# Turning all four q tiles on VectorE through DRAM, two beats later, in an attention and FFN kernel

## The chip, the cores and the metric

The kernel runs on one core of a Trainium2 chip. The metric is device time in microseconds (us) of one execution, lower is better. A core has TensorE (matrix products, PE in the profile, its weight loads PEld), VectorE (DVE), ScalarE (ACT), GpSimd (POOL) and SyncE (SP, here an issuer of DMAs). Each engine works through its own list of instructions in order; between engines the kernel sets semaphores by hand.

## The reference, cut to what matters

For each of 16 batches x is 128 x 1024 and the context 128 x 1024 (channels by positions), with 8 heads of 64.

```python
xn = layernorm(x)                                    # over the 1024 positions
q  = softmax(Wq @ xn, over the 64 channels of a head) * 64 ** -0.5
k  = softmax(Wk @ ctx, over the positions)
out = Wo @ (context of k and Wv @ ctx, applied to q) + bo
x  = x + out / norm(out over the 128 channels) * g * sqrt(128)
x  = x + ffn(layernorm(x))                           # gated lookup in 256 slots
```

## The kernel before, in words

About the first four fifths of the time are a pipeline of batches. `PERIODS` = 19 periods b run over every engine's list, each of four beats i = 0 to 3. In period b the keys of batch b are made, the queries of p = b-1, and older batches o = b-2 and e = b-3 are finished; the order on each engine is written out by hand in the loops at L672 (TensorE), L908 (ScalarE), L1133 (GpSimd) and L1417 (VectorE).

A beat on VectorE: `k_turn` (L1217, a block transpose of the exponentials of keys), `k_maximum` (L1210, straight from the PSUM buffer `k_slot`), `q_reciprocal` (L1242 `qsum`, L1246 `qrec`) for the queries one tile back, in two of four beats `q_block_turn` (L1255), and `q_shift` (L1229 `qm`, L1235). Between `q_shift` and `q_reciprocal` of a tile ScalarE does `q_exponential` (L798); after `q_reciprocal` GpSimd does `q_scale` (L1056). In beat 0 VectorE also makes the mean and variance of x (`x_statistics`, L1196, L1200), from which GpSimd's `rstd_pow` (L1039 to L1046) makes scale and bias for `x_layernorm`.

A q tile must be turned (queries down, channels across) before the output product. Tiles 0 and 1 (`BY_BLOCKS`) are turned in blocks of 32 by VectorE into `qt`, written to DRAM by one DMA on SP (`q_out`, L413) and read back by four DMAs that ScalarE issues (`q_in`, L814). Tiles 2 and 3 (`BY_PE`) are turned by TensorE (`q_turn`, L501) into the PSUM buffer `turn` and copied by ScalarE (`q_copy`, L803).

Then `o_pair` (L548) makes the output of two position tiles in `ob`; ScalarE copies it (`o_copy`, L824) and sums squares (`o_square`, L834, four small instructions, into the one buffer `l2`); GpSimd's `norm_scale` makes 1/norm from `l2` (L1067 `l2c`, L1069 `rn`) and scales (L1071 `o_sb`); TensorE turns it back (`o_turn`, L559); ScalarE takes it from PSUM (`o_scale`, L843); GpSimd adds it to x (`residual`, L1077); ScalarE and GpSimd make the second layernorm's numbers (`square_sum` L851, `rstd2_pow` L1089 to L1098). SP also moves the turned keys, sixteen DMAs for a half (`move_k`, L405, `ekT<-kt`). TensorE's other work in a beat is `k_tile` and `q_pair` (L475 to L477), `g_part` (L517) and `m_product` (L526). In the last two periods the steps of the FFN (`hidden_step`) begin.

One wait matters below: the first lines of `o_square`, and where the count `rn_pow` that it waits for is made, in `norm_scale`:

```python
act.wait_ge(o_copied, 2 * b + half + 1)
wait(act, rn_pow, b)
...
nc.gpsimd.tensor_tensor(rn[:, :], l2c[:, :], half_neg[:, 0:J], ALU.pow).then_inc(rn_pow, 1)
```

Of the kernel before, what the change touches and what calls it, by code (L numbers as in the profile page):

```python
# [49 lines left out]


def turned_by_pe(b, i):

    return len(BY_PE) * b + sum(t <= i for t in BY_PE)


def attention_ffn_kernel(nc, x, ctx_rows, ctx_cols, WqT_raw, WkT_raw, Wv_rows, WoT_rows, bo_row, g_col, Wuq_cols,
# [3 lines left out]
    with ctx:  # L61
# [46 lines left out]
        rstd = sb("rstd", [P, 1])
        nb = sb("nb", [P, 1])
        mr = sb("mr", [P, 1])  # L110
        mr2 = sb("mr2", [P, 1])
# [19 lines left out]
        q_turned = nc.dram_tensor("q_turned", (2, P, QUAD, T * P), F32, kind="Internal").ap()  # L131
# [340 lines left out]
        def _(pe):  # L472
# [24 lines left out]
            def q_turn(b, i):  # L497
                pe.wait_ge(q_mul, 4 * b + i + 1)
                for t in range(T):
                    for n in range(2):  # L500
                        last = nc.tensor.transpose(turn[:, (2 * t + n) * P:(2 * t + n + 1) * P],  # L501
# [1055 lines left out]
```

## Time and profile before

| | us |
|---|---|
| median of 3 runs | 637.53 (637.11 to 642.76) |
| the profiled execution | 638.21, span 636.4, mean granted TensorE clock 0.99 |
| busy in the span: PE, DVE | 598.8, 540.2 |
| busy in the span: ACT, POOL | 419.1, 409.8 |
| chain that ended last, shares | PE 36%, DVE 25%, POOL 16%, issue 14% |

The table's busy times are sums over the whole span. The rows further down show single instructions: start and duration in us from the start of the span, the engine (with q for its queue, where a DMA is issued), the line of the kernel and the operation, what it writes <- what it reads, and in brackets how long the engine stood idle before it and whom it waited for. Starts follow each other in less than a duration where an engine overlaps the end of one instruction with the next.

### The profile page before, as it was taken

How to read it: one execution, taken by the hardware profiler on the slowest of the kernel's cores; microseconds unless marked ns; L12 is line 12 of the kernel's file. 1: busy time of each engine (PE TensorE's matmuls, PEld its weight loads, DVE VectorE, ACT ScalarE, POOL GpSimd, SP SyncE). 2: the span in 40 equal slices, each digit the busy share in tenths (PEclk: the TensorE clock that was granted, in tenths of full speed). 3: DMA queues.
4: the chain of work that ended last, by engine and by line, in shares of the span. 5: the costliest groups of instructions: out<-in, count | busy, mean ns of one | idle time of the engine just before them, and what ended most of it. 6: DMA issues, size and time to landing. Idle time of an engine off the chain costs nothing.

```text
span 636.4 us, 11451 instructions
## 1 busy us (share of the span) xinstructions
PE 598.8 (94%) x3718; PEld 517.3 (81%) x3718; DVE 540.2 (85%) x721; ACT 419.1 (66%) x864; POOL 409.8 (64%) x421
## 2 busy tenths in 40 slices
PE   4989999999999999999999999999997799999896
PEld 3768888888888888888888888888886799998574
DVE  5999998989989898989898989899985635756897
ACT  5556657667667676767676676676683556774783
POOL 4964476777676778777777777776673536421394
PEclk9999999999999999999999999999998899999899
DMA  8849695867778684959595858675582500000056
GB/s 300 230 137 242 183 221 167 208 185 193 192 184 213 161 226 140 252 157 238 152 239 163 217 167 208 184 195 162 143 251 43 169 15 2 2 2 0 35 231 264
DMA packets 63530, 106.11 MB, mean 167 GB/s; under 512 B 11392, under 2 KB 43680, under 8 KB 61168
## 3 DMA queue, kind: packets, MB, share of 16 engines
q1 hardware_dynamic: 53216, 84.84, 46.1%
q10 hardware_dynamic: 9360, 18.09, 12.5%
q0 software_dynamic: 896, 2.45, 1.3%
q8 instruction: 30, 0.49, 0.3%
q14 instruction: 28, 0.23, 0.2%
HBM read 46.62 MB, written 25.17 MB: 113 GB/s over the span
## 4 chain that ended last, share of the span: by engine, by line
PE 36%; DVE 25%; POOL 16%; issue 14%; DMA 3%; SPq 3%; ACT 2%; DVEq 0%; POOLq 0%; ACTq 0%
DVE qsum L1242 7%; PE ob L548 7%; DVE kt L1217 5%; DVE qm L1229 5%; POOL ctx_lo L1033 4%; PE gm L604 4%; PE turn L604 4%; PE gm L517 4%; POOL qs_sb L1056 4%; POOL o_sb L1071 3%; POOL rn L1069 3%; SPq L405 3%; DVE qt L1255 3%; DMA ekT<-kt 2%; PE turn L559 2%
## 5 line engine op out<-in xcount | busy, mean ns | idle before, releaser
L1056 POOL TENSOR_TENSOR qs_sb<-qs_sb,qrec 128x1024 f32<-128x1024 f32 x64 | 121.9, 1905 | 126.0 <-DVE qrec L1246 125.9
L548 PE MATMUL ob<-mt_sb,q_hd 128*128 128x128 f32 x1024 | 127.4, 278 | 4.5 <-POOL mt_sb L1062 2.8
L548 PEld LDWEIGHTS ob<-mt_sb,q_hd 128*128 128x128 f32 x1024 | 122.6, 193 | 9.3 <-issue 6.4
L517 PE MATMUL gm<-ekT,ctxT 128*128 128x256 f32 x512 | 120.6, 384 | 4.7 <-DMA ekT<-kt 4.7
L517 PEld LDWEIGHTS gm<-ekT,ctxT 128*128 128x128 f32 x512 | 97.5, 192 | 22.3 <-DMA ekT<-kt 7.6
L788 ACT ACTIVATE ek<-k_slot,nkm 128x1024 f32<-128x1024 f32 x62 | 69.1, 1114 | 61.5 <-DVE nkm L1210 61.4
L798 ACT ACTIVATE qs_sb<-qs_sb 128x1024 f32<-128x1024 f32 x64 | 67.9, 1061 | 51.3 <-DVE qs_sb L1235 50.9
L1210 DVE TENSOR_REDUCE nkm<-k_slot 128x1 f32<-128x1024 f32 x62 | 74.1, 1194 | 25.1 <-PE k_slot L477 24.9
L1242 DVE TENSOR_REDUCE qsum<-qs_sb 128x16 f32<-128x1024 f32 x64 | 77.1, 1205 | 4.8 <-ACT qs_sb L798 3.7
L1235 DVE TENSOR_TENSOR qs_sb<-q_slot,qm 128x1024 f32<-128x1024 f32 x64 | 78.3, 1224 | 2.2
L1217 DVE STREAM_TRANSPOSE kt<-ek 128x1024 f32<-128x1024 f32 x64 | 79.0, 1234 | 0.8 <-DMA ekT<-kt 0.8
L1229 DVE TENSOR_REDUCE qm<-q_slot 128x16 f32<-128x1024 f32 x64 | 76.0, 1187 | 1.3 <-PE q_slot L477 1.1
L475 PE MATMUL k_slot<-ctx_hi,WkT_hi 128*128 128x512 f32 x124 | 54.5, 439 | 8.9 <-DVE ctx_lo L1408 7.2
L475 PE MATMUL q_slot<-WqT_hi,xn_hi 128*128 128x512 f32 x128 | 53.0, 414 | 0.8 <-DVE qs_sb L1235 0.8
L477 PE MATMUL q_slot<-WqT_lo,xn_hi 128*128 128x512 f32 x128 | 50.2, 392 | 0.0
L476 PE MATMUL q_slot<-WqT_hi,xn_lo 128*128 128x512 f32 x128 | 50.0, 390 | 0.0
L477 PE MATMUL k_slot<-ctx_lo,WkT_hi 128*128 128x512 f32 x124 | 49.3, 397 | 0.0
L476 PE MATMUL k_slot<-ctx_hi,WkT_lo 128*128 128x512 f32 x124 | 49.0, 396 | 0.0
L1050 POOL TENSOR_TENSOR xn_lo<-xn,xn_hi 128x1024 fp32r<-128x1024 f32 x16 | 38.3, 2392 | 4.3 <-ACT xn_hi L782 4.3
L1255 DVE STREAM_TRANSPOSE qt<-qs_sb 128x1024 f32<-128x1024 f32 x32 | 38.0, 1186 | 0.0
L834 ACT ACTIVATE junk<-o_sb 128x128 f32<-128x128 f32 x128 | 37.6, 299 | 0.0
L803 ACT COPY q_hd<-turn 128x1024 f32<-128x1024 f32 x32 | 31.9, 998 | 8.1 <-PE turn L501 8.1
(208 smaller groups left out, 1290.8 us busy)
## 6 DMA issues: line engine op xcount, KB each, us to landing
ekT<-kt SPq DMA_DIRECT2D x496, 64.0 KB, 3.1
q_turned<-qt SPq DMA_DIRECT2D x16, 1024.0 KB, 4.8
q_hd<-q_turned ACTq DMA_DIRECT2D x64, 256.0 KB, 6.0
ctx_in<-ctx_rows SPq DMA_DIRECT2D x16, 512.0 KB, 6.2
x_all<-x SPq DMA_DIRECT2D x16, 512.0 KB, 4.8
ctxT<-ctx_cols SPq DMA_DIRECT2D x16, 512.0 KB, 6.2
out<-q_hd SPq DMA_DIRECT2D x15, 512.0 KB, 2.6
Wuq_in<-Wuq_cols ACTq DMA_DIRECT2D x1, 1280.0 KB, 6.4
```

The lines of the kernel that those rows point to most:

```text
L475: nc.tensor.matmul(dst, lhs[0], rhs[0], start=True, stop=False)
L476: nc.tensor.matmul(dst, lhs[1], rhs[0], start=False, stop=False)
L477: return nc.tensor.matmul(dst, lhs[0], rhs[1], start=False, stop=True)
L517: last = nc.tensor.matmul(gm[:, cols], ctxT[:, b % 2, j, :], ekT[:, 2 * half:2 * half + 2, :, j * BLK:(j + 1) * BLK], start=(j == 0), stop ...
L548: last = nc.tensor.matmul(ob[:, (j % 4) * C:(j % 4 + 1) * C], q, mt_sb[:, b % 2, t, :], start=(t == 0), stop=(t == T - 1))
L788: nc.scalar.activation(ek[:, i % 2, :], k_psum(b, i)[:, :], ACT.Exp, bias=nkm[:, i:i + 1], accum_out=ksum[:, b % 2, i:i + 1]).then_inc(k_e ...
L1056: nc.gpsimd.tensor_tensor(e, e, qrec[:, i % 2, :].unsqueeze(2).broadcast_to([P, PAIR, DH]), ALU.mult).then_inc(q_mul, 1)
L1210: V.tensor_reduce(nkm[:, i:i + 1], k_psum(b, i)[:, :], AX, ALU.max, negate=True).then_inc(k_max, 1)
L1217: V.transpose(kt[:, i, :], ek[:, i % 2, :]).then_inc(k_T, 1)
L1229: V.tensor_reduce(qm[:, :], q, AX, ALU.max).then_inc(q_max, 1)
L1235: V.tensor_tensor(qs_sb[:, i % 2, :].rearrange("p (m d) -> p m d", d=DH), q, qm[:, :].unsqueeze(2).broadcast_to([P, PAIR, DH]), ALU.subtra ...
L1242: V.tensor_reduce(qsum[:, :], qs_sb[:, i % 2, :].rearrange("p (m d) -> p m d", d=DH), AX, ALU.add).then_inc(q_sum, 1)
```

## The change

All four q tiles are turned in blocks by VectorE and go through DRAM in two pairs (h = 0: tiles 0 and 1, h = 1: tiles 2 and 3), each with its own write and its own four reads; `qt` is shared by the pairs. `q_turn` and `q_copy` go. The output pairs run two beats later (pairs 0 and 1 in beats 2 and 3, pairs 2 and 3 in beats 0 and 1 of the next period), and what follows them moves too: `o_copy`, `o_square`, `norm_scale` (now in GpSimd's beat 0, for f = b-4), `o_turn`, `o_scale`, `residual`, `square_sum`, `rstd2_pow`. The sum and the sum of squares of x come from ScalarE (`x_sum`, `x_square`) for batches 2 to 15, with a negated mean by GpSimd (`x_negate`), in place of VectorE's `x_statistics`; x is loaded one period earlier. Small single columns share one tile. The diff, cut to its core (12 spaces of indentation left out):

```diff
-def q_out(b):
-    sp.wait_ge(q_blocks, 2 * b + 2)
-    wait(sp, q_back, 16 * QUAD * (b - 1))
-    sp.dma_start(q_turned[b % 2].rearrange("p q x -> p (q x)"),
-                 qt[:, :, :].rearrange("p i x -> p (i x)")).then_inc(q_written, 16)
+def q_out(b, h):
+    sp.wait_ge(q_blocks, 4 * b + 2 * h + 2)
+    wait(sp, q_back[h], 16 * QUAD * (b - 1))
+    sp.dma_start(q_turned[b % 2, h].rearrange("p q x -> p (q x)"),
+                 qt[:, :, :].rearrange("p i x -> p (i x)")).then_inc(q_written[h], 16)
 def ffn_tables():
...
         load_ctxT(b)
     if has(b):
         move_k(b, 0)
     if has(b - 1):
-        q_out(b - 1)
+        q_out(b - 1, 0)
     if 2 <= b + 2 < B:
         load_ctx(b + 2)
     if has(b):
         move_k(b, 1)
     if b == B:
         ffn_tables()
+    if has(b - 1):
+        q_out(b - 1, 1)
...
-def o_pair(b, n_out):
-    i = OUT_ORDER[n_out]
-    if i in BY_BLOCKS:
-        pe.wait_ge(q_back, 16 * QUAD * (b + 1))
-    else:
-        pe.wait_ge(q_copied, turned_by_pe(b, i))
-    if n_out == 0:
+def o_pair(b, i):
+    if i % 2 == 0:
+        pe.wait_ge(q_back[i // 2], 16 * QUAD * (b + 1))
+        wait(pe, o_copied, 2 * b + i // 2)
+    if i == 0:
         pe.wait_ge(mt_biased, b + 1)
         if b == 0:
             pe.wait_ge(score_ready, 2)
-    if n_out % 2 == 0:
-        wait(pe, o_copied, 2 * b + n_out // 2)
...
         if b == 1 and i == 1:
             value_products(1)
             router_product()
-        qb, qi = (p, i - 2) if i >= 2 else (o, i + 2)
-        if has(qb) and qi in BY_PE:
-            if qb == 0 and qi == BY_PE[0]:
-                pe.wait_ge(u_done, 1)
-                pe.wait_ge(ident_in, 16)
-            take_turn(q_turn, qb, qi)
-            q_turn(qb, qi)
         if has(p):
             if p == 0 and i == 0:
...
                 m_product(p)
-        if has(e) and i == 2:
-            take_turn(o_turn, e)
-            o_turn(e)
-        if has(o):
-            o_pair(o, i)
+        at, n = (o, i - 2) if i >= 2 else (e, i + 2)
+        if has(at):
+            o_pair(at, n)
+        if has(f) and i == 1 or b == B + 2 and i == 3:
+            take_turn(f if i == 1 else B - 1)
+            o_turn(f if i == 1 else B - 1)
         if b == 0 and i == 3:
             head_products()
...
+def x_sum(b):
+    act.wait_ge(x_in[b % 4], 16 * (b // 4 + 1))
+    wait(act, x_negated, b - 2)
+    wait(act, l2_sum, 2 * (b - 4) + 1)
+    wait(act, x_squared, b - 2)
+    wait(act, ssq_done, b - 5)
+    nc.scalar.activation(junk[:, :, :].rearrange("p j c -> p (j c)"), X[:, b, :], ACT.Copy,
+                         accum_out=xsum).then_inc(x_summed, 1)
+def x_square(b):
+    act.wait_ge(x_negated, b - 1)
+    wait(act, x_ve, b)
+    wait(act, l2_sum, 2 * (b - 4) + 2)
+    act.wait_ge(x_summed, b - 1)
+    nc.scalar.activation(junk[:, :, :].rearrange("p j c -> p (j c)"), X[:, b, :], ACT.Square, bias=nm1,
+                         accum_out=xsq).then_inc(x_squared, 1)
...
-def q_copy(b, i):
-    act.wait_ge(q_T, turned_by_pe(b, i))
-    wait(act, o_prod, 4 * (b - 1) + OUT_ORDER.index(i) + 1)
-    nc.scalar.copy(q_hd[:, i, :], turn[:, :]).then_inc(q_copied, 1)
...
-def q_in(b):
-    if b == 0:
+def q_in(b, h):
+    if b == 0 and h == 0:
         act.wait_ge(k_weights, 2)
         act.wait_ge(q_weights, 2)
         act.wait_ge(u_prod, 1)
-    act.wait_ge(q_written, 16 * (b + 1))
-    wait(act, o_prod, 4 * b)
+    act.wait_ge(q_written[h], 16 * (b + 1))
+    wait(act, o_prod, 4 * (b - 1) + 2 * h + 2)
     for q in range(QUAD):
-        nc.scalar.dma_start(q_hd[q * BLK:(q + 1) * BLK, 0:2, :].rearrange("r i (a x) -> r (i a) x", a=2),
-                     q_turned[b % 2, :, q, :].rearrange("(a r) x -> r a x", a=QUAD)).then_inc(q_back, 16)
+        nc.scalar.dma_start(q_hd[q * BLK:(q + 1) * BLK, 2 * h:2 * h + 2, :].rearrange("r i (a x) -> r (i a) x", a=2),
+                            q_turned[b % 2, h, :, q, :].rearrange("(a r) x -> r a x",
...
     act.wait_ge(o_copied, 2 * b + half + 1)
     wait(act, rn_pow, b)
     wait(act, l2_sum, 2 * b + half)
-    first = 2 * OUT_ORDER[2 * half]
-    for j in range(first, first + 4):
-        last = nc.scalar.activation(junk[:, j % 4, :], o_sb[:, b % 2, j, :], ACT.Square,
+    if half == 0:
+        wait(act, x_squared, min(b + 2, B - 2))
+    else:
+        wait(act, x_summed, min(b + 3, B - 2))
+        wait(act, ssq_done, min(b - 1, RESIDUAL_BY_VECTOR))
+    for j in range(4 * half, 4 * half + 4):
+        last = nc.scalar.activation(junk[:, j, :], o_sb[:, b % 2, j, :], ACT.Square,
                                     accum_out=l2[:, j:j + 1])
...
     act.wait_ge(x1_done, b + 1)
     act.wait_ge(nm2_done, b + 1)
     wait(act, ve2_done, b)
-    nc.scalar.activation(o_sb[:, b % 2, :, :].rearrange("p j c -> p (j c)"), X[:, b, :], ACT.Square,
+    act.wait_ge(l2_sum, 2 * (b + 2) + 1)
+    nc.scalar.activation(junk[:, :, :].rearrange("p j c -> p (j c)"), X[:, b, :], ACT.Square,
                          bias=nm2[:, b % 2:b % 2 + 1], accum_out=ssq[:, :]).then_inc(ssq_done, 1)
...
 for b in range(PERIODS):
-    p, o, e = b - 1, b - 2, b - 3
+    p, o, e, f = b - 1, b - 2, b - 3, b - 4
     for i in range(4):
-        if i == 0 and o == B - 1:
-            q_copy(o, 2)
         if i == 0 and has(o):
             mt_scale(o)
         if i == 0 and has(e):
+            o_copy(e, 0)
+        if i == 2 and has(e):
             o_copy(e, 1)
-        if i == 2 and has(o):
-            o_copy(o, 0)
+        if i == 2 and 0 <= f < RESIDUAL_BY_VECTOR:
+            o_scale(f)
         if i == 1 and has(o):
-            q_in(o)
-        qb, qi = (p, i - 1) if i else (o, 3)
-        if has(qb):
-            q_exponential(qb, qi)
-        qb, qi = (p, i - 2) if i >= 2 else (o, i + 2)
-        if has(qb) and qi in BY_PE and (qb, qi) != (B - 1, 2):
-            q_copy(qb, qi)
+            q_in(o, 0)
+        if i == 3 and has(o):
+            q_in(o, 1)
         if b == B + 1 and i == 0:
             act.wait_ge(q_prod, 4 * B)
             act.wait_ge(m_prod, B)
             hT_high(0, 0)
             h_scale(1, 1)
+        qb, qi = (p, i - 1) if i else (o, 3)
+        if has(qb):
+            q_exponential(qb, qi)
         if 0 < b < B:
             k_exponential(b, i)
         if i == 1 and 0 < b and has(b + 1):
             ctx_high(b + 1)
         if i == 0 and has(e):
+            o_square(e, 0)
+        if i == 3 and has(e) and e < B - 1 or i == 2 and e == B - 1:
             o_square(e, 1)
-        if i == 3 and has(o):
-            o_square(o, 0)
-        if i == 3 and 0 <= e < RESIDUAL_BY_VECTOR:
-            o_scale(e)
         if i == 1 and 0 < b < B:
             x_layernorm(b)
-        if i == 1 and 0 <= e - 1 < RESIDUAL_BY_VECTOR:
-            square_sum(e - 1)
+        if i == 1 and 0 <= f - 1 < RESIDUAL_BY_VECTOR:
+            square_sum(f - 1)
         if i == 2:
             if has(p):
                 g_copy(p)
             if 0 < b < B:
                 x_high(b)
+            if 1 < b + 1 < B:
+                x_sum(b + 1)
+        if i == 3 and 1 < b + 1 < B:
+            x_square(b + 1)
         if b == 1 and i == 0:
             act.wait_ge(u_prod, 1)
             nc.scalar.mul(U[:, :, :].rearrange("p h c -> p (h c)"), turn[:, :],
...
+def x_negate(b):
+    pool.wait_ge(x_summed, b - 1)
+    nc.gpsimd.tensor_scalar(mv1[:, b, 0:1], xsum, 1.0 / N, None, ALU.mult).then_inc(x_mean, 1)
+    wait(pool, x_squared, b - 2)
+    pool.wait_ge(x_mean, b - 1)
+    nc.gpsimd.tensor_scalar(nm1, mv1[:, b, 0:1], -1.0, None, ALU.mult).then_inc(x_negated, 1)
 def rstd_pow(b):
-    pool.wait_ge(x_mv, b + 1)
     wait(pool, x_norm, b)
-    nc.gpsimd.tensor_scalar(ve[:, :], mv1[:, b, 1:2], LN_EPS, None, ALU.add).then_inc(x_ve, 1)
+    if b < 2:
+        pool.wait_ge(x_mv, b + 1)
+        nc.gpsimd.tensor_scalar(ve[:, :], mv1[:, b, 1:2], LN_EPS, None, ALU.add).then_inc(x_ve, 1)
+    else:
+        pool.wait_ge(x_squared, b - 1)
+        nc.gpsimd.tensor_scalar(ve[:, :], xsq, 1.0 / N, LN_EPS, ALU.mult, ALU.add).then_inc(x_ve, 1)
     pool.wait_ge(x_ve, b + 1)
     nc.gpsimd.tensor_tensor(rstd[:, :], ve[:, :], half_neg[:, 0:1], ALU.pow).then_inc(x_rstd, 1)
...
 for b in range(PERIODS):
-    p, o, e = b - 1, b - 2, b - 3
+    p, o, e, f = b - 1, b - 2, b - 3, b - 4
     for i in range(4):
         if i == 0 and has(o):
             mt_bias(o)
-        if i == 0 and 0 <= e - 1 < RESIDUAL_BY_VECTOR:
-            residual(e - 1)
+        if i == 3 and 0 <= f < RESIDUAL_BY_VECTOR:
+            residual(f)
+        if i == 3 and 1 < b + 1 < B:
+            x_negate(b + 1)
         if i == 3 and 0 < b < B:
...
             q_scale(qb, qi)
         if i == 0 and 0 < b < B:
             rstd_pow(b)
-        if i == 0 and has(e - 1) and e - 1 >= RESIDUAL_BY_VECTOR:
-            rstd2_pow(e - 1)
-        if i == 3 and 0 <= e - 1 < RESIDUAL_BY_VECTOR:
-            rstd2_pow(e - 1)
+        if i == 0 and has(f):
+            norm_scale(f)
+        if i == 0 and has(f - 1) and f - 1 >= RESIDUAL_BY_VECTOR:
+            rstd2_pow(f - 1)
+        if i == 2 and 0 <= f - 1 < RESIDUAL_BY_VECTOR:
+            rstd2_pow(f - 1)
         if i == 1 and b > 0 and has(b + 1):
             ctx_low(b + 1)
-        if i == 1 and has(e):
-            norm_scale(e)
+        if b == B + 2 and i == 3:
+            norm_scale(B - 1)
         if b == B and i == 3:
             for half in range(2):
                 pool.wait_ge(k_moved[half], moved(B))
             nc.gpsimd.memset(q_rows[:, :, BOT:P], 1.0).then_inc(query_ones, 1)
         if early_step(b, i) > 0:
             hidden_sum(early_step(b, i))
-rstd2_pow(B - 1)
+for b in range(B - 2, B):
+    rstd2_pow(b)
...
 def q_block_turn(b, i):
-    n = BY_BLOCKS.index(i)
     dve.wait_ge(q_mul, 4 * b + i + 1)
-    wait(dve, q_written, 16 * b)
+    wait(dve, q_written[1 - i // 2], 16 * (b + i // 2))
     turned = qt[:, :, :].rearrange("p i x -> p (i x)").rearrange("p (q t i n x) -> p i n t q x", q=QUAD, t=T,
                                                                  i=2, n=2)
-    V.transpose(turned[:, n, :, :, :, :],
+    V.transpose(turned[:, i % 2, :, :, :, :],
                 qs_sb[:, i % 2, :].rearrange("p (n t q x) -> p n t q x", n=2, t=T,
                                              q=QUAD)).then_inc(q_blocks, 1)
...
             q_reciprocal(qb, qi)
-        if i == 0 and 0 < b < B:
+        if i == 0 and b == 1:
             x_statistics(b)
         if i == 1:
             if has(p):
                 k_scale(p)
         qb, qi = (p, i - 2) if i >= 2 else (o, i + 2)
-        if has(qb) and qi in BY_BLOCKS:
+        if has(qb):
             q_block_turn(qb, qi)
         if has(p):
             q_shift(p, i)
-        if i == 2 and has(e) and e >= RESIDUAL_BY_VECTOR:
-            residual(e)
-        if i == 3 and has(e) and e >= RESIDUAL_BY_VECTOR:
-            statistics(e)
+        if i == 2 and has(f) and f >= RESIDUAL_BY_VECTOR:
+            residual(f)
+        if i == 3 and has(f) and f >= RESIDUAL_BY_VECTOR:
+            statistics(f)
         if b == 0 and i == 3:
             dve.wait_ge(side_in, 16 * 2)
             V.tensor_scalar_mul(bo_bc[:, :], bo_bc[:, :], 0.5).then_inc(bo_halved, 1)
```

## Rows read from the trace of the kernel before

**Rows 1.** Chain that ended last, 240 to 345: start, us, engine, tile, line

```profile
303.88 1.91 POOL o_sb L1071
```

**Rows 2.** Timeline, VectorE, 299 to 331 (columns as told above)

```profile
299.66 1.23 DVE L1217 STREAM_TRANSPOSE kt<-ek 128x1024 f32<-128x1024 f32 x1
...
310.19 1.23 DVE L1210 TENSOR_REDUCE nkm<-k_slot 128x1 f32<-128x1024 f32 x1 [1.95 <-PE k_slot L477]
311.34 1.21 DVE L1242 TENSOR_REDUCE qsum<-qs_sb 128x16 f32<-128x1024 f32 x1
312.58 0.25 DVE L1246 RECIPROCAL qrec<-qsum 128x16 f32<-128x16 f32 x1
312.75 1.19 DVE L1255 STREAM_TRANSPOSE qt<-qs_sb 128x1024 f32<-128x1024 f32 x1
...
318.49 1.20 DVE L1242 TENSOR_REDUCE qsum<-qs_sb 128x16 f32<-128x1024 f32 x1
...
329.70 1.23 DVE L1217 STREAM_TRANSPOSE kt<-ek 128x1024 f32<-128x1024 f32 x1
```

**Rows 3.** Timeline, GpSimd, 299 to 331

```profile
301.78 0.26 POOL L1067 TENSOR_SCALAR l2c<-l 128x8 f32<-128x8 f32 x1
302.13 1.68 POOL L1069 TENSOR_TENSOR rn<-l2c,half_neg 128x8 f32<-128x8 f32 x1
...
312.91 1.90 POOL L1056 TENSOR_TENSOR qs_sb<-qs_sb,qrec 128x1024 f32<-128x1024 f32 x1 [2.93 <-DVE qrec L1246]
...
320.13 1.91 POOL L1056 TENSOR_TENSOR qs_sb<-qs_sb,qrec 128x1024 f32<-128x1024 f32 x1
322.12 0.23 POOL L1039 TENSOR_SCALAR ve<-mv 128x1 f32<-128x1 f32 x1
...
323.35 0.23 POOL L1046 TENSOR_SCALAR nb<-mr 128x1 f32<-128x1 f32 x1
```

**Rows 4.** Timeline, ScalarE, 299 to 331 (ACTq: a DMA issue)

```profile
301.02 1.06 ACT L798 ACTIVATE qs_sb<-qs_sb 128x1024 f32<-128x1024 f32 x1
...
318.97 0.83 ACTq L814 DMA_DIRECT2D q_hd<-q_turned  x2
...
320.33 0.46 ACTq L814 DMA_DIRECT2D q_hd<-q_turned  x1
```

**Rows 5.** Timeline, ScalarE, 436 to 441

```profile
438.74 1.11 ACT L788 ACTIVATE ek<-k_slot,nkm 128x1024 f32<-128x1024 f32 x1 [0.30 <-DVE nkm L1210]
439.11 0.98 ACTq L814 DMA_DIRECT2D q_hd<-q_turned  x2
```

**Rows 6.** Line 413 between 434 and 435: the write, issue to landing

```profile
L413 SPq DMA_DIRECT2D q_turned<-qt x1: 332/332/332, 434.1 to 434.1; - x1
...
DMA to landing us min/median/max: 3.8/3.8/3.8
```

**Rows 7.** Timelines, TensorE, 299 to 331 and 455 to 530

```profile
301.54 3.61 PE L517 MATMUL gm<-ekT,ctxT 128*128 128x256 f32 x16
...
308.53 0.47 PE L475 MATMUL k_slot<-ctx_hi,WkT_hi 128*128 128x512 f32 x1
...
310.00 0.40 PE L475 MATMUL q_slot<-WqT_hi,xn_hi 128*128 128x512 f32 x1
...
482.48 5.41 PE L517 MATMUL gm<-ekT,ctxT 128*128 128x256 f32 x16 [3.77 <-DMA ekT<-kt]
...
499.51 2.94 PE L548 MATMUL ob<-mt_sb,q_hd 128*128 128x128 f32 x16 [2.83 <-POOL mt_sb L1062]
...
509.64 2.05 PE L548 MATMUL ob<-mt_sb,q_hd 128*128 128x128 f32 x16 [1.10 <-ACT q_hd L803]
```

**Rows 8.** Three stretches: us, busy (instructions) by engine, PEclk, DMA share, GB/s

```profile
483.00:486.00 3.00, 3.00 (x9) 2.43 (x8) 0.93 (x1) 0.00 (x0) 0.00 (x0) 0.56 0.00 0
500.00:503.00 3.00, 3.00 (x17) 2.80 (x17) 1.86 (x2) 3.00 (x10) 0.61 (x1) 0.57 0.39 157
510.00:515.00 5.00, 5.00 (x42) 5.00 (x41) 1.23 (x1) 2.37 (x3) 3.93 (x3) 1.00 0.06 13
```

More of the change, by code:

```diff
@@ L26 @@
 MOVED = 16 * QUAD * QUAD
-BY_BLOCKS = (0, 1)
-BY_PE = tuple(i for i in range(4) if i not in BY_BLOCKS)
-OUT_ORDER = BY_PE + BY_BLOCKS
 RESIDUAL_BY_VECTOR = B - 3
@@ L103, in attention_ffn_kernel @@
         nm2 = sb("nm2", [P, 2])
-        ssq = sb("ssq", [P, 1])
-        ve = sb("ve", [P, 1])
-        ve2 = sb("ve2", [P, 1])
         l2c = sb("l2c", [P, J])
[L108 to L111, printed above, removed]
+        singles = sb("singles", [P, 10])
+        ssq, ve, ve2, rstd, nb, mr, mr2, xsum, nm1, xsq = (singles[:, n:n + 1] for n in range(10))
         att = ExitStack()
@@ L128, in attention_ffn_kernel @@
         att.close()
[L131 removed]
+        q_turned = nc.dram_tensor("q_turned", (2, 2, P, QUAD, T * P), F32, kind="Internal").ap()
         stage = q_hd[:, :, :].rearrange("p t n -> p (t n)")
@@ L242, in attention_ffn_kernel @@
         log_rel_in = sem("log_rel_in")
-        x_in = [sem(f"x_in{k}") for k in range(2)]
+        x_in = [sem(f"x_in{k}") for k in range(4)]
         ctx_loaded = sem("ctx_loaded")
@@ L296, in attention_ffn_kernel @@
         q_mul = sem("q_mul")
-        q_T = sem("q_T")
-        q_copied = sem("q_copied")
         q_blocks = sem("q_blocks")
-        q_written = sem("q_written")
-        q_back = sem("q_back")
+        q_written = [sem(f"q_written{h}") for h in range(2)]
+        q_back = [sem(f"q_back{h}") for h in range(2)]
         o_back = sem("o_back")
@@ L495, in q_pair @@
                 last.then_inc(q_prod, 1)
[L497 to L501, printed above, removed]
-                                                   qs_sb[:, i % 2, n * HALF + t * P:n * HALF + (t + 1) * P],
-                                                   ident[:, :])
-                last.then_inc(q_T, 1)
             def g_part(b, half, js):
@@ L819, in o_copy @@
                 wait(act, x1_done, b - 1)
-                if half == 0:
-                    wait(act, ssq_done, min(b - 1, RESIDUAL_BY_VECTOR))
                 wait(act, l2_sum, 2 * b)
-                first = 2 * OUT_ORDER[2 * half]
-                nc.scalar.copy(o_sb[:, b % 2, first:first + 4, :],
+                nc.scalar.copy(o_sb[:, b % 2, 4 * half:4 * half + 4, :],
                                ob[:, :].rearrange("p (j c) -> p j c", c=C)).then_inc(o_copied, 1)
@@ L1230, in q_shift @@
                 dve.wait_ge(q_max, n + 1)
-                if n >= 2 and (n - 2) % 4 in BY_PE:
-                    dve.wait_ge(q_T, turned_by_pe((n - 2) // 4, (n - 2) % 4))
-                if n >= 2 and (n - 2) % 4 in BY_BLOCKS:
-                    dve.wait_ge(q_blocks, len(BY_BLOCKS) * ((n - 2) // 4) + BY_BLOCKS.index((n - 2) % 4) + 1)
+                wait(dve, q_blocks, n - 1)
                 V.tensor_tensor(qs_sb[:, i % 2, :].rearrange("p (m d) -> p m d", d=DH), q,
```

54 lines of the change are left out of this document (25 added, 29 removed).

## The prediction

> **What bounds the kernel now.** I read four views in this order: the chain that ended last, to see which engines hand work to each other; VectorE's own timeline, to see whether it ever stands still; the timelines of ScalarE and GpSimd, for what each link of a chain costs; and the stretches in which TensorE's granted clock falls. The profiled execution took 638.21 us, its span 636.4; the median of the runs is 637.53, so a sum against the profiled execution is lowered by 0.7 at the end.
>
> Batches overlap, and the loop over periods b repeats: from one `k_turn` of beat 2 to the same one a period later are 30.04 us (299.66 to 329.70) [rows 2]. VectorE is the fullest engine in it. It stands still at one place, 1.95 us ahead of `k_maximum` in beat 3, for TensorE's `k_tile` [rows 2]. The chain shows why TensorE is late there: in beat 2 it waits for GpSimd's `norm_scale` (o_sb, to 305.78) before `o_turn` [rows 1], and `o_pair` and `k_tile` are queued behind that. So a period is VectorE's own work, 28.1 us, plus that stall of 1.95.
>
> **The change, part by part.** I write b for the period, p, o, e, f for b-1 to b-4.
>
> *VectorE.* Two more block turns a period (tiles 2 and 3), 1.19 us each [rows 2]; away goes `x_statistics`. A beat with a block turn and no wait runs from one `qsum` to the next in 7.15 us (311.34 to 318.49) [rows 2]; afterwards all four beats are of that kind, 4 x 7.15 = 28.6. TensorE loses both `q_turn`s, and its beat 2 no longer holds `o_turn`, so the stall of 1.95 before `k_maximum` should go but for a few tenths. Were this all, a period would fall by 1.4 us.
>
> *What is hidden.* ScalarE gives up two `q_copy` and takes `x_sum` and `x_square`: in beats 2 and 3, behind exponentials with slack of some tenths of a us, at nothing. GpSimd's `x_negate` and its other steps that move to other beats: GpSimd waits for VectorE in most beats, nothing, with one exception below. The second pair's write on SP is queued behind the sixteen `move_k` DMAs of the half before it and can leave about when the turn of tile 3 ends; the next turn into the same buffer comes over 5 us later, and the whole buffer (both tiles at once, as now) was written in 3.8 where I looked [rows 6]. Nothing, and up to 0.5 a period if traffic slows it.
>
> *The exception: one wait in ScalarE's queue.* `o_square` waits for `rn_pow >= b` of its batch, that is for `norm_scale` of the batch before, because both use the one buffer `l2`. Now both `o_square`s find that long done. In the changed kernel `o_square(e, 0)` is issued in beat 0 of period b, and the batch before e is f, whose `norm_scale(f)` moves to GpSimd's beat 0 of the same period, behind `q_scale(o, 3)` and `rstd_pow(b)`. `q_scale(o, 3)` in turn needs VectorE's `qrec` of that same beat. Behind the blocked `o_square` stand, in ScalarE's order, the four DMA issues of `q_in(o, 0)` and then `q_exponential(p, 0)`, and for the last VectorE waits in beat 1 with `qsum`. So there is a closed loop through three engines, from `qsum` of beat 0 to `qsum` of beat 1:
> - `qsum` start to `qrec` start 1.24 (311.34 to 312.58) [rows 2], on to `q_scale` 0.33 (312.91) [rows 3]: 1.57;
> - `q_scale` to GpSimd's next instruction 1.99 (320.13 to 322.12) [rows 3];
> - `rstd_pow`, four small instructions, 322.12 to 323.35 + 0.23 [rows 3]: 1.46, and 0.1 to the next;
> - `l2c` and `rn`, 301.78 to 302.13 + 1.68 [rows 3]: 2.03, and 0.1 to reach ScalarE;
> - ScalarE hands out the squares and then issues the four `q_in` DMAs. Now the same sequence lies behind a `k_exponential`: the first DMA is issued 0.37 after that one starts (438.74 to 439.11) [rows 5], and the four issues last from 318.97 to 320.33 + 0.46 [rows 4]: 0.37 + 1.82 = 2.19, and 0.1 to the next;
> - `q_exponential` 1.06 [rows 4] and 0.05 to `qsum`.
>
> The sum is 1.57 + 1.99 + 1.56 + 2.13 + 2.29 + 1.11 = 10.65, where VectorE's own work between the two places is 7.15. VectorE is stalled for 3.5 us in beat 1. A period then takes 10.65 + 3 x 7.15 = 32.1 us against 30.04: 2.1 more. The other beats cannot win it back, since they hold nothing but VectorE's work.
>
> The length of the ScalarE link is the one that is open. If the DMA issues delayed nothing, four squares at about 0.3 each (1.2 us) would stand in place of 2.19, and the period were 31.1. Against that: in a later period the write that `q_in` waits for left at 434.1 and landed 3.8 later, at 437.9 [rows 6], yet the first `q_in` DMA was issued only at 439.11, behind the `k_exponential` ahead of it that had to wait for its data until 438.74 [rows 5]. ScalarE's queue does not run past an instruction that waits, so I take 2.19. The Trainium skill, "Perfetto Trace Analysis", section "DVE / Act Engine Instruction", says that the sequencer pushes an engine instruction into a wait queue and is free for the next one while the semaphores are awaited. By that rule the DMAs would be issued during the wait, and the period would be the shorter one; the rows just named speak against it here.
>
> *TensorE's clock.* The stall opens a gap for TensorE. `k_exponential(b, 1)` (1.11 [rows 5]) follows the late `q_exponential`, then `k_tile(b, 2)` (1.47, 308.53 to 310.00 [rows 7]) ends about 2.6 us after `qsum`; the next product needs `q_shift` of beat 1, some 5.0 after `qsum`. So TensorE idles about 2.4 us in one piece. Around gaps of 3.77 and 2.83 us [rows 7] the granted clock stood at 0.56 and 0.57 in the stretch that followed, so it was mostly at the lower of its two levels, 1.2 GHz; after one of 1.10 (at 509) [rows 7] it kept 1.00, the level of 2.4 GHz [rows 8]. A gap of 2.4 lies between these, nearer to 2.83. The price of one fall: sixteen matmuls of `g_part` took 5.41 where they take 3.61 [rows 7], 1.8 more, and these stand in beat 2, where TensorE has no slack. Bounds: no period or all twelve; I take three, 5.4 us, because the rows show falls beside longer gaps only.
>
> *How many periods.* The wait bites where e >= 1 and the products of keys still run: b = 4 to 15, twelve periods, 12 x 2.1 = 25.2. In period 3 there is no batch f and the period falls by 1.4. Period 16 waits for DMAs of `ekT` anyway (TensorE 3.77 idle [rows 7]), which covers most of the loop. In the last two periods `o_turn` of the last batch comes a beat later, and the block in ScalarE's queue holds up the first transposed hidden rows; on the other side the turns of the last tiles no longer need TensorE and ScalarE. I put these at 0, bounds -4 and +7, one loop less its cover on either side.
>
> Sum: 638.2 + 25.2 - 1.4 + 5.4 = 667.4; less 0.7 for the median: **667 us**.
>
> **The rivals.**
> 1. *The queue runs ahead* (the DMA issues are no part of the loop). Period 31.1: 12 x 1.06 - 1.4 = 11.3, three clock falls 5.4: 638.2 + 16.7 - 0.7 = 654. For it: the squares themselves need only 1.2 us. Against it: the issue at 439.11.
> 2. *The clock falls in every period.* 12 x 1.8 in place of 3 x 1.8: 667 + 16 = 683. For it: a gap of 2.4 with another short gap ahead of it is close to 2.83. Against it: each fall in the rows stands beside a longer gap.
> 3. *The loop does not close, the kernel is faster.* The place is `o_square(e, 0)`: were `norm_scale(f)` done before `qrec` of beat 0 is needed, ScalarE would pass it, VectorE would be the bound at 28.6, and thirteen periods would win 1.4 each: 638.2 - 18.7 - 0.7 = 619, or some 622 with a few tenths of stall left in each. It decides at a ScalarE link so short that the loop takes 7.15 in all, 3.5 less than the sum. Against it: the four GpSimd links alone, 1.57 + 1.99 + 1.56 + 2.13 = 7.25, already exceed it.
> 4. *No change:* the loop takes 8.6 us, so that stall and gain cancel. No row makes it so short.
>
> **How the numbers follow.** The forecast (3.5 us stall, a few clock falls) has 0.63, its own range 658 to 677; rival 1 has 0.13, rival 2 has 0.12, rival 3 has 0.08, no change 0.04. The range reaches from rival 1 with a good tail (654 - 4 = 650) to rival 2 with a bad one (683 + 5 = 688). Within 1% of the time before, 631 to 644, is about what a measurement here cannot tell from no change: slower 0.88, same 0.04, faster 0.08.
>
> **What would show it.** Right: in the profile after, ScalarE's `o_square` after beat 0 waits some 6 us for GpSimd's `rn`; VectorE's `qsum` waits about 3.5 us for `q_exponential` once a period; `k_turn` repeats every 32 us in periods 4 to 15 and faster in period 3; the 1.95 us wait of `k_maximum` is gone or a few tenths. Wrong: a period of 28.6 to 29 with `rn` done ahead of `o_square` (rival 3); `q_in` DMAs issued while ScalarE waits (rival 1); granted clock well below 1.00 across the middle (rival 2); or a wait of the block turn for the pair's write, which I put at nothing.

## The result, and the profile after

| | before | after |
|---|---|---|
| median of the runs, us | 637.96 (637.11 to 642.76, 4 runs) | 697.49 (694.77 to 698.38, 4 runs) |
| ratio to before, 95% interval | | 1.091 (1.088 to 1.095) |
| span of the profiled execution, us | 636.4 | 695.3 |
| start of period 4 to start of period 16, us | 359.6 | 407.7 |
| from there to the end, us | 171.0 | 181.3 |

The change costs 59.5 us; 667 was forecast, with a range to 688. Here and below a period runs from the `k_turn` of one beat 0 to the next. Of the 58.9 us between the spans, periods 4 to 15 hold 48.1, everything from period 16 on 10.4, and the first three periods with the start 0.4.

The page of the kernel after, its span and its engines (busy us, share of the span, instructions):

```profile
span 695.3 us, 11139 instructions
...
PE 597.0 (86%) x3462; PEld 501.4 (72%) x3462; DVE 561.2 (81%) x711; ACT 420.5 (60%) x888; POOL 417.3 (60%) x449
```

VectorE is busy for 81% of the span, where it was busy for 85% before. Its waits, 140 to 480 us (line, waited for: us in total, times, longest), say what it stands for:

```profile
DVE qsum L1234 <- ACT qs_sb L778: 34.0, 11, 4.3
DVE nkm L1205 <- PE k_slot L468: 17.1, 10, 1.8
DVE qt L1246 <- DMA q_turned<-qt: 1.2, 3, 0.7
```

The first was forecast, 3.1 us a time. The second is the wait of [rows 2], which the change was to remove: it is back with 1.7 us, for another reason. One period of VectorE's timeline (start, us, engine, line, operation; in brackets the idle time before it and what ended it), against [rows 2]:

```profile
309.20 1.23 DVE L1212 STREAM_TRANSPOSE kt<-ek 128x1024 f32<-128x1024 f32 x1
...
311.46 1.20 DVE L1234 TENSOR_REDUCE qsum<-qs_sb 128x16 f32<-128x1024 f32 x1
312.70 0.25 DVE L1238 RECIPROCAL qrec<-qsum 128x16 f32<-128x16 f32 x1
...
321.92 1.22 DVE L1234 TENSOR_REDUCE qsum<-qs_sb 128x16 f32<-128x1024 f32 x1 [2.92 <-ACT qs_sb L778]
...
337.01 1.23 DVE L1205 TENSOR_REDUCE nkm<-k_slot 128x1 f32<-128x1024 f32 x1 [1.75 <-PE k_slot L468]
...
343.04 1.24 DVE L1212 STREAM_TRANSPOSE kt<-ek 128x1024 f32<-128x1024 f32 x1
```

The period is 33.84 us instead of 30.04. GpSimd in beat 0 of it, against [rows 3]:

```profile
313.03 1.90 POOL L1046 TENSOR_TENSOR qs_sb<-qs_sb,qrec 128x1024 f32<-128x1024 f32 x1 [3.25 <-DVE qrec L1238]
315.02 0.19 POOL L1029 TENSOR_SCALAR singles<-singles 128x1 f32<-128x1 f32 x1
...
316.54 0.26 POOL L1057 TENSOR_SCALAR l2c<-l 128x8 f32<-128x8 f32 x1
316.87 1.67 POOL L1059 TENSOR_TENSOR rn<-l2c,half_neg 128x8 f32<-128x8 f32 x1
```

And ScalarE, which starts `o_square` 0.08 us after that `rn` ends, against [rows 4]:

```profile
318.62 0.31 ACT L811 ACTIVATE junk<-o_sb 128x128 f32<-128x128 f32 x1 [5.84 <-issue]
...
318.90 0.32 ACTq L789 DMA_DIRECT2D q_hd<-q_turned  x1
...
319.74 1.05 ACTq L789 DMA_DIRECT2D q_hd<-q_turned  x2
320.83 1.06 ACT L778 ACTIVATE qs_sb<-qs_sb 128x1024 f32<-128x1024 f32 x1 [0.92 <-issue]
```

That is the loop as it was written down. TensorE in beats 2 and 3 of the same period, and two stretches of it (us, busy, PEclk, DMA share, GB/s), against [rows 7, 8]:

```profile
324.34 0.39 PE L468 MATMUL k_slot<-ctx_lo,WkT_hi 128*128 128x512 f32 x1
327.11 0.50 PE L466 MATMUL q_slot<-WqT_hi,xn_hi 128*128 128x512 f32 x1 [2.38 <-DVE qs_sb L1227]
...
329.55 4.25 PE L499 MATMUL gm<-ekT,ctxT 128*128 128x256 f32 x16
```

```profile
322.00:324.00 2.00, 1.77 (x13) 1.00 1.06 241
...
327.00:330.00 3.00, 2.89 (x8) 0.57 0.99 337
```

TensorE stands for 2.38 us, and in the stretch behind that the granted clock is 0.57, mostly the 1.2 GHz level. The products of q and the first part of `g_part` go slowly, `k_tile` of beat 3 is late, and `k_maximum` waits 1.75 for it. This happens in each of the periods 5 to 15, eleven times, and not in period 4, which takes 32.2 us. Yet period 4 has the same gap, 2.38 us, and behind it the clock stays at 1.00:

```profile
124.20 0.47 PE L466 MATMUL q_slot<-WqT_hi,xn_hi 128*128 128x512 f32 x1 [2.38 <-DVE qs_sb L1227]
```

```profile
124.00:128.00 4.00, 3.80 (x17) 1.00 0.98 369
```

So the length of the gap alone does not decide; why period 4 was spared stays open.

### The profile page after: what moved, and what is told of

It reads as the page before. It is cut to its first block, busy times and chain, and to the rows that moved or that the text cites. A ratio compares the mean times of both kernels' runs of the same rounds, so it can differ in the third digit from the quotient of the medians.

```text
span 695.3 us, 11139 instructions
## 1 busy us (share of the span) xinstructions
PE 597.0 (86%) x3462; PEld 501.4 (72%) x3462; DVE 561.2 (81%) x711; ACT 420.5 (60%) x888; POOL 417.3 (60%) x449
## 3 DMA queue, kind: packets, MB, share of 16 engines
q10 hardware_dynamic: 18576, 34.87, 21.9%
## 4 chain that ended last, share of the span: by engine, by line
PE 34%; issue 27%; DVE 15%; ACT 11%; DMA 4%; ACTq 3%; SPq 3%; POOL 2%; DVEq 0%; POOLq 0%
PE gm L499 9%; PE ob L524 4%; ACT junk L811 4%; PE turn L577 4%; DVE qm L1224 3%; DVE qsum L1234 3%; ACTq L789 3%; SPq L394 3%; DVE qs_sb L1227 2%; ACT qs_sb L778 2%; DVE nkm L1205 2%; PE q_slot L466 2%; PE gm L577 2%; ACT mt_sb L837 2%; PE q_slot L468 2%
## 5 line engine op out<-in xcount | busy, mean ns | idle before, releaser
L499 PE MATMUL gm<-ekT,ctxT 128*128 128x256 f32 x512 | 127.7, 400 | 1.6 <-DMA ekT<-kt 1.4
L499 PEld LDWEIGHTS gm<-ekT,ctxT 128*128 128x128 f32 x512 | 105.0, 206 | 21.6 <-DMA ekT<-kt 3.3
L466 PE MATMUL q_slot<-WqT_hi,xn_hi 128*128 128x512 f32 x128 | 58.4, 456 | 58.8 <-DVE qs_sb L1227 58.8
L466 PEld LDWEIGHTS q_slot<-WqT_hi,xn_hi 128*128 128x128 f32 x128 | 26.0, 203 | 80.4 <-issue 76.5
L1246 DVE STREAM_TRANSPOSE qt<-qs_sb 128x1024 f32<-128x1024 f32 x64 | 76.9, 1202 | 5.8 <-DMA q_turned<-qt 5.8
L466 PE MATMUL k_slot<-ctx_hi,WkT_hi 128*128 128x512 f32 x124 | 54.5, 440 | 16.5 <-ACT ek L768 9.2
L468 PE MATMUL q_slot<-WqT_lo,xn_hi 128*128 128x512 f32 x128 | 55.7, 435 | 0.0
L467 PE MATMUL q_slot<-WqT_hi,xn_lo 128*128 128x512 f32 x128 | 55.4, 433 | 0.0
L774 ACT COPY g_sb<-gm 128x512 f32<-128x512 f32 x16 | 9.4, 586 | 51.8 <-PE gm L499 51.8
```

What stands on the lines that cost most here:

```text
L466: nc.tensor.matmul(dst, lhs[0], rhs[0], start=True, stop=False)
L467: nc.tensor.matmul(dst, lhs[1], rhs[0], start=False, stop=False)
L468: return nc.tensor.matmul(dst, lhs[0], rhs[1], start=False, stop=True)
L499: last = nc.tensor.matmul(gm[:, cols], ctxT[:, b % 2, j, :], ekT[:, 2 * half:2 * half + 2, :, j * BLK:(j + 1) * BLK], start=(j == 0), stop ...
```

## Experiments

All times are medians, with the ratio to the kernel before on the same chip. Because the first period differs between the executions (27.6 to 33.8 us, see the experiments on x's statistics), I also give the length of the twelve periods 4 to 15 in the profiled execution; before 359.6, after 407.7.

**The clock alone.** Is the second wait the clock's?

```diff
-                        k_tile(b, i)
+                        k_tile(b, i, 2 if i == 2 and b >= 4 else 1)   # computed that many times over
```

> The changed kernel, in which TensorE computes the third k tile of each batch from 4 on twice over, into the same place: 1.36 us of work put into the gap of 2.35 us ahead of the third q tile, from which VectorE reads only later. The loop stays. Theory A (the gap brings the clock down, and the lower clock costs 1.8 us a period behind it): the gap is 1.0 us, no clock falls in periods 5 to 15, k_max no longer waits in beat 3, the period is 34.05 - 1.8 = 32.2 and the time 697.5 - 11 x 1.8 = 678. Rival D (the clock falls of themselves every 34 us, whatever TensorE did before, or their cost is hidden by VectorE's work): 693 to 700.

Measured 685.71 us, ratio 1.072 (1.069 to 1.075); the twelve periods 391.6. TensorE in that gap, VectorE's waits, and the stretch 140 to 450 (us; busy us and instructions of PE, PEld, DVE, ACT, POOL; PEclk, DMA share, GB/s):

```profile
292.23 0.47 PE L466 MATMUL q_slot<-WqT_hi,xn_hi 128*128 128x512 f32 x1 [1.03 <-DVE qs_sb L1227]
...
293.69 3.62 PE L499 MATMUL gm<-ekT,ctxT 128*128 128x256 f32 x16
```

```profile
DVE qsum L1234 <- ACT qs_sb L778: 25.8, 9, 3.6
DVE qt L1246 <- DMA q_turned<-qt: 6.0, 9, 1.5
DVE nkm L1205 <- PE k_slot L468: 0.3, 2, 0.2
```

```profile
140.00:450.00 310.00, 281.90 (x1661) 234.85 (x1658) 272.45 (x275) 199.60 (x443) 213.75 (x236) 1.00 0.91 242
```

More work on TensorE makes the kernel faster. With the gap at 1.03 the clock is 1.00 throughout, `g_part` takes 3.62 instead of 4.25, `k_maximum` waits for next to nothing, and the wait of `qsum` is about as it was (2.9 us a time, 3.1 before). The twelve periods lose 16.1 us, of which the median shows 11.8 (this execution's first period was 5.0 longer). Rival D falls. What is left, 391.6 against 359.6, is the loop with little else. In eight of its twelve periods ScalarE's part of the loop, from the first square to `q_exponential`, is longer than the 2.21 above, 2.38 to 3.51, mostly because the four issues last longer; one of them:

```profile
315.98 0.31 ACT L811 ACTIVATE junk<-o_sb 128x128 f32<-128x128 f32 x1 [5.85 <-issue]
...
317.09 2.28 ACTq L789 DMA_DIRECT2D q_hd<-q_turned  x2
319.42 1.06 ACT L778 ACTIVATE qs_sb<-qs_sb 128x1024 f32<-128x1024 f32 x1 [2.15 <-issue]
```

The waits of the block turn for the write (6.0 us) cost nothing here: they stand in beat 0, inside the loop, and `qsum` waits the less behind them.

**The loop, opened.** Theory A against the write as the true end of ScalarE's wait.

```diff
-        l2 = sb("l2", [P, J])
+        l2 = sb("l2", [P, 2, J])
-                wait(act, rn_pow, b)
+                wait(act, rn_pow, b - 1)
-                        accum_out=l2[:, j:j + 1]
+                        accum_out=l2[:, b % 2, j:j + 1]
```

(`norm_scale` reads `l2[:, b % 2, :]`.)

> The changed kernel with two buffers for the sums of squares (l2 by the parity of the batch), so that o_square(e, 0) waits for rn of the batch before and no more for that of the batch just ahead of it. Nothing else is changed. Theory A (a closed loop VectorE, GpSimd, ScalarE costs 3.4 us a period from period 4 on, and the 2.35 us gap that it leaves on TensorE ahead of the third q tile costs another 1.8 by a lower clock): the semaphore wait of 6.9 us on ScalarE goes, the qsum of beat 1 no longer waits, no clock falls in periods 5 to 15, the period is 28.6 to 29.3 us against 34.0; 697.5 - 11 x 5.0 - 3.2 = 639 us, between 632 and 645. Rival B (the write of the pair to DRAM would end ScalarE's wait at the same place anyway, because q_in stands ahead of q_exp): the wait moves to the first q_in, the period stays above 33, 685 to 697 us.

Measured 656.38 us, ratio 1.028 (1.025 to 1.030); the twelve periods 366.4. VectorE's waits in 140 to 450, and that stretch:

```profile
DVE qt L1246 <- DMA q_turned<-qt: 15.3, 12, 2.6
DVE nkm L1205 <- PE k_slot L468: 0.6, 2, 0.5
```

```profile
140.00:450.00 310.00, 285.55 (x1698) 239.65 (x1697) 290.66 (x294) 215.75 (x468) 226.68 (x252) 0.99 1.02 258
```

The wait of `qsum` is gone, 34.0 us (140 to 480) to none, and with it all falls of the clock from 140 to 455 but one: 41 us of the 59.5 go with the loop. Rival B falls: the period is 30.5 on average, not above 33. But the time is 656 and not 639. Neither theory had said what takes the place: the block turn now waits for the write of the other pair, 15.3 us in twelve times, and the DMA engines' share is 1.02, that is, full. Nothing covers these waits any more: period 15, which has none, takes 28.9 us, and period 4, with one of 2.64, takes 31.7. The kernel before had 0.73 there and the kernel after 0.84.

**Two links, shortened.** `o_square` waits for the last reader of `l2` instead of `rn`; and, in another kernel, `q_in(o, 0)` stands behind `q_exponential(p, 0)`.

```diff
-                wait(act, rn_pow, b)
+                wait(act, l2_clamped, b)
```

> The changed kernel, with one wait of o_square set on l2_clamped of the batch before (the last reader of l2) instead of rn_pow, one GpSimd instruction later. Theory A: the loop is shorter by one rn (1.68 us) and still closed: 10.5 to 8.8 us against 7.15 of VectorE's own work, so the wait of qsum falls from 3.4 to 1.7 us, and TensorE's gap from 2.35 to 0.65. If the clock then stays up, the period is 34.05 - 1.7 - 1.8 = 30.5 and the time 697.5 - 11 x 3.5 - 1.7 = 657; if it falls all the same, 32.35 and 697.5 - 12 x 1.7 = 677. Rival B (the write to DRAM ends the wait): no change, 690 to 697.

```diff
-                    if i == 1 and has(o):
-                        q_in(o, 0)
...
                     if has(qb):
                         q_exponential(qb, qi)
+                    if i == 1 and has(o):
+                        q_in(o, 0)
```

> The changed kernel with the four issues of q_in(o, 0) in beat 1 put behind q_exp(p, 0) on ScalarE instead of ahead of it. Theory A: the four issues (1.9 us) leave the loop, which is 8.6 us against 7.15; the wait of qsum falls from 3.4 to about 1.5, and with the clock up the period is 30.3 (time 655), with the clock still falling 32.15 (time 675). Rival C (the queue takes the four issues ahead while ScalarE still waits or computes, so they are no part of the loop): no change, 693 to 700.

The first: 666.80 us (1.043, 1.039 to 1.048), the twelve periods 377.5, most of them 30.9. The loop in one of these:

```profile
303.16 1.20 DVE L1234 TENSOR_REDUCE qsum<-qs_sb 128x16 f32<-128x1024 f32 x1
...
312.33 1.22 DVE L1234 TENSOR_REDUCE qsum<-qs_sb 128x16 f32<-128x1024 f32 x1 [1.33 <-ACT qs_sb L778]
```

That is 9.17 instead of 10.46, 1.3 of the 1.7 of `rn`; the rest is lost because the four issues last longer (ScalarE's part is 2.68 instead of 2.21). In 140 to 450 the clock falls twice. The median is 10 above my 657: the two periods with a fall take 33.5 and 34.1, and most others stay at 30.9 where 30.5 was written.

The second: 679.64 us (1.063, 1.058 to 1.068), the twelve periods 381.7, most of them 31.2 to 31.9. The loop in one of the best:

```profile
309.44 1.20 DVE L1234 TENSOR_REDUCE qsum<-qs_sb 128x16 f32<-128x1024 f32 x1
...
318.86 1.22 DVE L1234 TENSOR_REDUCE qsum<-qs_sb 128x16 f32<-128x1024 f32 x1 [1.41 <-ACT qs_sb L778]
```

Rival C falls, but only half of the 1.9 us came: the loop is 9.42, and against the 32.2 of the kernel without falls the best periods gain 1.0. The rows of ScalarE above say why. The issues run beside the four squares, and `q_exponential` waits only the last 0.92 us for them (`[0.92 <-issue]`); the squares remain when the issues are gone. And 17.6 us of waits for the write appear; most of them stand in beat 0, where the loop covers them, but the longest, 4.3 us, stands in the longest period, 33.6.

**The transfers.** With the loop open, from batch 2 on a quarter of the second pair's bytes.

```diff
+                rows = slice(0, BLK if h and b >= 2 else P)
-                sp.dma_start(q_turned[b % 2, h] ..., qt[:, :, :] ...)
+                sp.dma_start(q_turned[b % 2, h, rows] ..., qt[rows, :, :] ...)
+                    (each of the four reads: 32 x 512 elements instead of four times that)
```

> The kernel with two buffers of sums (656 us), in which from batch 2 on the second pair of q tiles is moved only by a quarter: 32 of 128 rows are written to DRAM, and each of the four reads brings a quarter of its bytes. That leaves three quarters of that pair's values out; all other work is the same. Theory E (with the loop open, the DMA engines are full: 95% busy, 1.3 us a period of the block turn waiting for the write of the other pair, and that holds the period at 30.5 where VectorE's own work is 28.7): the wait for the write goes, the period is 28.6 to 29.2, 656 - 12 x 1.5 = 638, between 632 and 644. Rival F (not the bytes but the order of the issues on the queue of SyncE sets when a pair is written, or another engine is at its limit): 650 to 657.

Measured 637.45 us, ratio 0.997 (0.993 to 1.000); the twelve periods 349.9, eleven of them 28.9. All of VectorE's waits in 140 to 450, and that stretch:

```profile
DVE nkm L1210 <- PE k_slot L469: 0.2, 1, 0.2
```

```profile
140.00:450.00 310.00, 297.25 (x1802) 253.29 (x1799) 305.67 (x313) 227.28 (x499) 237.30 (x262) 1.00 0.82 216
```

VectorE is busy 305.7 of 310 us: this is close to the period that the prediction wrote down for the change without its loop, 28.6. So three quarters of the second pair's bytes cost 16.5 us in twelve periods (366.4 - 349.9) once nothing slower hides them. Rival F falls.

**x's statistics.** Put back on VectorE with the loop closed, and with it open; and moved alone, in the kernel before.

```diff
-                    if i == 0 and b == 1:
+                    if i == 0 and 0 < b < B:
                         x_statistics(b)
```

(with `x_sum`, `x_square`, `x_negate` and their waits taken out)

> The changed kernel with x's statistics back on VectorE, in beat 0, as before the change; the loop stays closed. Theory A (VectorE's work between qsum of beat 0 and qsum of beat 1 lies under the loop of 10.5 us, which has 3.4 us of room): the 1.4 us that VectorE gets back cost nothing, 693 to 702 us, and the wait of qsum in beat 1 is shorter by about as much. Rival G (VectorE is the bound, and the statistics' move did save): 697.5 + 12 x 1.4 = 714.

> The kernel with two buffers of sums (656 us), with x's statistics back on VectorE. Theory E (the transfers hold the period at 30.5, so that VectorE's 1.4 us are covered up to some 0.5): 656 to 664. Rival G (VectorE is the bound there, and the statistics' move saves what it takes off it): 656 + 12 x 1.4 = 673 or more.

Closed: 693.62 us (1.089, 1.081 to 1.096), 4 below the changed kernel, within what the runs of either spread; the twelve periods are 398.9 against 407.7. VectorE's own work fills some of the stall (21.9 us of waits of `qsum` in nine times, 2.4 each); TensorE's gap is then about 2.0 in most periods, and in 140 to 455 the clock falls five times instead of nine. Open: 660.38 us (1.037, 1.029 to 1.044), 4 above; the twelve periods are 365.5 against 366.4, and the block turn's waits for the write shrink from 15.3 us to 0.4: VectorE now works where it waited. In both, what the change takes off VectorE buys nothing in these periods. Rival G falls twice.

> The kernel before the change, with x's statistics alone moved to ScalarE and GpSimd as the change does it, and nothing else of the change. Theory G (VectorE is the bound of the kernel before, and nothing closes a loop here, for the sums of squares are read in the same period, beats away from the next): the period falls from 30.04 by the 1.4 to 1.5 us of the statistics to 28.6, in 14 periods, 637.5 - 14 x 1.4 = 618, between 615 and 625. Rival H (another limit stands close behind VectorE, the transfers or TensorE, as in the kernel with two buffers of sums): 630 to 638.

Alone: 630.50 us, ratio 0.987 (0.982 to 0.993), the twelve periods 347.6. The median lies in H's 630 to 638, and H names one limit rightly: in 140 to 450 VectorE waits 23.3 us for TensorE's `k_tile`, in 21 times, and the period is 28.9 and not G's 28.6. And 5.3 us are lost at the start: the first period is 33.1, where the kernel before has 27.8. So:

```diff
-                if 2 <= b + 2 < B:
-                    load_x(b + 2)
+                if 2 <= b + 1 < B:
+                    load_x(b + 1)
```

> The kernel before the change with x's statistics alone on ScalarE and GpSimd (630.5 us), with each load of x issued a period later, as in the kernel before. Its first period was 33.1 us against 27.8, 3.2 us of it TensorE waiting for the value weights. Theory L (the earlier load of x stands in the queue ahead of what the first period waits for): the first period is 28 to 29, 626 us, between 624 and 628. Rival M (when the value weights land differs from chip to chip and launch to launch, whatever is queued): no change, 629 to 632.

Measured 625.03 us, ratio **0.979 (0.975 to 0.983)**: faster than both kernels. The first period is 27.6, and the twelve periods are what they were (347.3), so theory L stands for this kernel. TensorE is the full engine, and VectorE waits for it in every period:

```profile
300.58 1.22 DVE L1246 TENSOR_REDUCE nkm<-k_slot 128x1 f32<-128x1024 f32 x1 [1.64 <-PE k_slot L476]
```

```profile
140.00:450.00 310.00, 309.73 (x1974) 272.61 (x1972) 282.21 (x290) 242.05 (x506) 237.75 (x260) 1.00 0.74 195
```

In nine of the ten profiled executions with x loaded a period early, one of each kernel, the first period was 31.6 to 33.8; in that of the changed kernel it was 28.8. Why that one escaped stays open.

**The tail.** With the loop open, the last batch's second pair a beat sooner.

```diff
+                    if i == 1 and e == B - 1:
+                        o_copy(e, 1)
+                        o_square(e, 1)
-                    if b == B + 2 and i == 3:
+                    if b == B + 2 and i == 2:
                         norm_scale(B - 1)
```

(`o_turn` likewise; `residual` and `statistics` of the last batch ahead of VectorE's last hidden step of the loop.)

> The kernel with two buffers of sums (656 us), in which the last batch's second output pair is handled a beat sooner: its copy and its squares on ScalarE stand ahead of the hidden step of that beat instead of behind it, and the norm on GpSimd, the turn on TensorE and the residual on VectorE follow in the next beat. Work and periods 1 to 16 are the same. Theory T (the output pairs' two beats of delay lengthen the tail, because the residual of the last batch ends it: the turn waits for GpSimd, which waits 4.6 us for ScalarE behind the hidden step): the last turn comes 4 to 5 us sooner and the tail is 173 us against 177.7, 652 us. Rival U (the tail is as long as TensorE's hidden products, which fill these waits anyway): 655 to 658.

Measured 653.28 us, ratio 1.024 (1.020 to 1.029). The median alone would speak for theory T, the trace does not: counted from the start of period 16 the last `o_sb` of `norm_scale` begins 5.7 us sooner and the last residual 3.5, but the last hidden rows 0.9 and the end 0.4 (177.3 against 177.7). The rest of the gain lies in the periods before. So rival U: something else fills the tail. TensorE does. From the first `hT_low` to the last hidden rows, first in the kernel before, then with the loop open:

```profile
501.10:574.30 73.20, 71.33 (x522) 70.13 (x521) 40.55 (x82) 49.71 (x98) 33.75 (x37) 0.98 0.07 16
```

```profile
511.20:592.80 81.60, 73.00 (x543) 71.14 (x541) 47.66 (x89) 50.30 (x107) 40.12 (x47) 1.00 0.17 47
```

Before, TensorE stands for 1.9 us in this stretch; afterwards it has 1.7 us more to do (80 `o_pair` products instead of 55, 24 turns instead of 16) and stands for 8.6. That the later output pairs bring both is read from these rows; no run here takes them back alone.

## Why the prediction was wrong

The direction and the first mechanism held; three terms were mis-sized, those of the clock and of the tail by most. In us between the spans: forecast 29.2 without the 0.7 to the median, measured 58.9.

| term | forecast | measured | where |
|---|---|---|---|
| loop, periods 4 to 15 | 25.2 | 32.0 | twelve periods without falls, 391.6 - 359.6 |
| falls of the clock | 5.4 | 16.1 | 407.7 - 391.6 |
| periods 1 to 3 and start | -1.4 | 0.4 | period 3 -0.5, periods 1 and 2 +1.7, start -0.8 |
| period 16 and tail | 0 | 10.4 | 181.3 - 171.0 |

1. *The loop: right, its size a little low.* 10.65 us from `qsum` to `qsum` was summed; 311.46 to 321.92 is 10.46. Each link stands in the rows above: 1.57, 1.99, 1.52, 2.08, 2.21 (318.62 to 320.83), 1.09. The period without falls was to be 32.1 and is 32.2 at its shortest, 32.6 on average. That 32.1 and 32.2 meet is in part luck: the loop came out 0.2 shorter than summed, and the other three beats take 21.8 where 3 x 7.15 = 21.45 was written. The average is higher because the four issues, put at one length, mostly last longer: in the kernel without falls ScalarE's part is 2.2 to 3.5, and the loop 10.44 to 11.76, 10.86 on average.
2. *Rival 1, the queue runs ahead: wrong.* The rule of the Trainium skill, "Perfetto Trace Analysis", section "DVE / Act Engine Instruction", was weighed there: the sequencer hands an instruction to a wait queue and is free for the next. ScalarE stands 5.84 us ahead of `o_square`, and not one of the four issues behind it leaves in that time; the first comes 0.28 after `o_square` has begun. In the trace the wait is an entry of its own in ScalarE's sequencer, of 6.94 us, so the rule does not apply to this wait. Once the square runs, the issues do run beside it; the rival's 31.1 is about what the kernel with the issues behind `q_exponential` reaches, 31.2.
3. *The clock: the step that failed.* "I take three, 5.4 us, because the rows show falls beside longer gaps only." The gap was sized well (2.4 against 2.34 to 2.38) and its price too (1.5 a fall measured, 1.8 forecast). But I had rows for 2.83 and for 1.10, none between, and then put a number between the bounds that no row gives. Eleven of the twelve gaps came with a fall, all but that of period 4. Rival 2 was this case, and at 683 it was the nearest; the tail and the loop carried the time past the range. That the answer follows from the length of the gap is not shown either: with the statistics back on VectorE, gaps of 1.95 to 2.05 had a fall in three cases of seven.
4. *The tail: the other step that failed, a term of 0 with bounds -4 to +7, measured +10.4.* With the loop open it is +6.8, with less moved +3.3, by one execution each. The later `o_turn` and the blocked queue in the tail were priced; that the last batches' products now run among the hidden products, where TensorE was 97% busy before, was not. What makes up the 3.6 between the closed and the open loop stays open.
5. *VectorE's saving: nearly right in size, and lost.* 28.6 us a period was written down for VectorE alone; 28.9 is what it takes where nothing slower stands above it (the second pair cut down), 1.1 less than 30.04. But that VectorE was the fullest engine before was misread. Over 140 to 450 of the kernel before TensorE is busy for 303.2 us and VectorE for 286.2:

```profile
140.00:450.00 310.00, 303.18 (x1902) 262.48 (x1902) 286.16 (x313) 215.18 (x454) 226.85 (x238) 1.00 0.73 192
```

   Where the statistics alone move, it is TensorE that holds the period at 28.9.
6. *The bound behind the loop: named, and priced at nothing.* The 3.8 us of one write, from which this was worked out, was the shortest of eleven between 140 and 480; their median is 4.8. A wait of the block turn for the pair's write stood among the signs that would prove the prediction wrong. The sum for rival 3, 619 to 622, took VectorE as the next limit all the same; the kernel with the loop open takes 656, for there the DMA engines are full first. In the changed kernel the loop hides most of that wait.

## What to carry to other kernels

When a wait repeats in every period, price what it opens on the other engines for every period too, as a case of its own, and take a number between none and all only if a row gives it. When a closed loop is opened, the next bound need not be an engine that was full before; here it was what the change had loaded more: look at the share of the DMA engines before trusting the engines' own sums. Of a change in several parts, time each part alone: here one of them was worth 2% by itself, and together with the others it was lost.
